# The aggregation pass of a graph-network layer: squares kept in PSUM and scanned first, stores issued in pairs, mask rows asked for at a group's head

## The reference, cut to what matters

```python
m = concat([h[dst], h[src]]) @ W_pre + b_pre
mean = segment_sum(m, dst) / deg
mean_sq = segment_sum(m * m, dst) / deg
std = sqrt(relu(mean_sq - mean * mean) + STD_EPS)
mn = segment_min(m, dst)
mx = segment_max(m, dst)
```

## Time and profile before

| | us |
|---|---|
| median of 3 runs | 4757.76 (4754.0 to 4763.07) |
| the profiled execution | 4755.44 |
| its span in the trace | 4753.5 |
| mean granted PE clock of the span | 0.706 |

### The profile page before, as it was taken

One profiled execution on the slowest core, in us unless ns is written; L12 is line 12 of the kernel. 1 busy time (PEld: TensorE's weight loads), 2 busy tenths in 40 slices (PEclk: granted clock), 3 DMA queues, 4 the chain that ended last, 5 costly groups with the idle time before them and its releaser, 6 DMA issues. The chain is left out here.

```text
span 4753.5 us, 79156 instructions
## 1 busy us (share of the span) xinstructions
PE 3229.7 (68%) x19497; PEld 2761.8 (58%) x19497; DVE 3212.5 (68%) x7496; ACT 2330.0 (49%) x4887; POOL 3360.5 (71%) x3428
## 2 busy tenths in 40 slices
PE   4888888887433334436566656665597888888886
PEld 3666666666433333335455555555465777777776
DVE  5888888887533333345677778777656676667677
ACT  4776666664200000003566666666535566666665
POOL 4777777774777777776777777777523777777774
PEclk7555555556766656667777777777798788888887
DMA  7333333331222222222677777777732333333333
GB/s 141 87 88 88 87 87 88 88 88 36 64 55 55 55 56 55 55 56 66 200 250 254 252 247 256 250 260 250 257 111 65 79 83 81 81 80 82 82 82 75
DMA packets 368299, 567.20 MB, mean 119 GB/s; under 512 B 107028, under 2 KB 171191, under 8 KB 367860
## 3 DMA queue, kind: packets, MB, share of 16 engines
q1 hardware_dynamic: 254190, 332.06, 21.5%
q0 software_dynamic: 106720, 227.64, 20.0%
q10 hardware_dynamic: 6950, 2.44, 0.2%
HBM read 328.98 MB, written 230.89 MB: 118 GB/s over the span
## 5 line engine op out<-in xcount | busy, mean ns | idle before, releaser
L2121 POOL DMA_INDIRECT m_G<-dr_tab,chunk_src x782 | 878.9, 1124 | 247.1 <-issue 238.0
L896 POOL DMA_INDIRECT e_G<-dr_tab,src_idx x830 | 792.6, 955 | 272.4 <-issue 233.5
L896 POOL DMA_INDIRECT v_G<-dr_tab,src_idx x830 | 789.4, 951 | 253.4 <-issue 245.6
L1899 POOL DMA_INDIRECT s_G<-dr_tab,chunk_src x760 | 717.3, 944 | 235.5 <-issue 226.7
L2007 PE MATMUL s_OUT<-s_G,s_S 128*128 x1664 | 378.0, 419 | 557.9 <-POOLq L1892 511.3
L2007 PEld LDWEIGHTS s_OUT<-s_G,s_S 128*128 128x128 f32 x1664 | 353.0, 323 | 582.6 <-issue 582.6
L2263 PE MATMUL m_BK<-eye,m_XT 128*128 128x128 f32 x3136 | 544.4, 342 | 170.2 <-ACT m_XB L2179 160.7
L1953 DVE TENSOR_TENSOR ACC<-ACC,s_OUT 128x129 f32 x832 | 241.4, 290 | 591.5 <-PE s_OUT L2007 474.1
L2263 PEld LDWEIGHTS m_BK<-eye,m_XT 128*128 128x128 f32 x3136 | 487.8, 181 | 217.1 <-ACT m_XB L2179 187.7
L1329 PE MATMUL e_OUT<-e_RH,e_S 128*128 128x144 f32 x1664 | 512.6, 477 | 1.9 <-DVE e_RH L1215 1.9
L2456 ACT COPY f_AT<-r_TP 128x512 f32<-128x512 f32 (+1 forms) x13 | 7.2, 554 | 943.9 <-PE r_TP L2478 943.9
(11 more groups left out here) (377 smaller groups left out, 7226.4 us busy)
## 6 DMA issues: line engine op xcount, KB each, us to landing
dr_ends<-m_XB SPq DMA_DIRECT2D x392, 512.0 KB, 4.4
e_LR<-dr_row_loc SPq DMA_DIRECT2D x104, 256.0 KB
v_LR<-dr_row_loc SPq DMA_DIRECT2D x104, 256.0 KB
m_SAME<-dr_row_same SPq DMA_DIRECT2D x98, 256.0 KB, 5.7
s_G<-dr_tab SPq DMA_DIRECT2D x1408, 0.5 KB
s_G<-dr_tab ACTq DMA_DIRECT2D x1408, 0.5 KB
e_G<-dr_tab,src_idx POOLq DMA_INDIRECT x830
v_G<-dr_tab,src_idx POOLq DMA_INDIRECT x830
```

Of the source, the lines that this page charges most:

```text
L896: pool.indirect_dma_start(out=out, out_offset=None, in_=table, in_offset=bass.IndirectOffsetOnAxis(ap=g["src_idx"][:, step:step + 1], axis ...
L1899: pool.indirect_dma_start(out=G[:, c % (RING * GROUP), 0:D], out_offset=None, in_=table[:, :], in_offset=bass.IndirectOffsetOnAxis(ap=g["c ...
L2121: pool.indirect_dma_start(out=G[:, k % Q, c % GROUP, :], out_offset=None, in_=table[:, :], in_offset=bass.IndirectOffsetOnAxis(ap=g["chunk ...
```

## The change

SQT moves from SBUF into PSUM, two banks, as one buffer where there were two. Room is made by two copy banks in place of three (`BANKS`), and by laying `UPTO` into the first of them. The squares are scanned first: the order of the parts becomes squares, sum, minimum, maximum (`TURNS`), and the semaphore counts are by place in that order (`i`) instead of by part (`m`). ACT makes `squares(k + 1)` between the copies of group `k`'s first and second part, where it made `squares(k + 2)` behind group `k`'s fourth. PE's order stays but that the `UPTO` products stand ahead of `turn(1)`. The four stores of a group go in two pairs: the first pair when the first half of the last part is copied, the second when the second half is. The mask row is asked for three groups ahead, at the group's head, once all scans of the group before are done, instead of four ahead after the group's own scans.

```diff
-    BANKS = 3
+    SUM, LEAST, MOST, SQUARES = range(PARTS)
+    TURNS = (SQUARES, SUM, LEAST, MOST)
+    BANKS = 2
...
-        SQT = fin.spare[:, 0:2 * SLOTS].rearrange("p (b c) -> p b c", b=2)
-        zero = fin.spare[:, 2 * SLOTS:2 * SLOTS + PARTS * D]
+        zero = fin.spare[:, 0:PARTS * D]
...
-        UPTO = ctx.enter_context(nc.psum_tensor(name + "UPTO", [P, 2, 3, TILES], F32))
+        SQT = ctx.enter_context(nc.psum_tensor(name + "SQT", [P, SLOTS], F32))
+        UPTO = BK[:, 0, 0:2 * 3 * TILES].rearrange("p (m c t) -> p m c t", m=2, c=3)
...
-                    if k + 4 < PICKS:
-                        sp.wait_ge(scanned, PARTS * (k + 1))
-                        same(k + 4)
+                    if 1 <= k and k + 3 < PICKS:
+                        sp.wait_ge(scanned, PARTS * k)
+                        same(k + 3)
                     for q in range(PAIRS):
-                        sp.wait_ge(xb_done, halves(k, PARTS - 1) + 2 * q + 2 if k + 1 < PICKS else halves(PICKS, 0))
+                        sp.wait_ge(xb_done, halves(k, PARTS - 1) + q // 2 + 1)
...
                 def resets(k):
                     act.wait_ge(same_in[k % 4], 16 * (k // 4 + 1))
-                    wait(act, scanned, PARTS * (k - 2) + 3)
+                    wait(act, scanned, PARTS * (k - 1))
...
                 def squares(k):
                     act.wait_ge(gt_done, k + 1)
-                    wait(act, scanned, PARTS * (k - 1))
-                    nc.scalar.activation(SQT[:, k % 2], GT[:, k % 2], ACT.Square).then_inc(sq_done, 1)
+                    wait(act, scanned, PARTS * (k - 1) + 1)
+                    nc.scalar.activation(SQT[:], GT[:, k % 2], ACT.Square).then_inc(sq_done, 1)
...
                 for k in range(PICKS):
-                    for m in range(PARTS):
-                        back(k, m)
+                    back(k, 0)
+                    if k + 1 < PICKS:
+                        squares(k + 1)
+                    for i in range(1, PARTS):
+                        back(k, i)
                     if k + 2 < PICKS:
-                        squares(k + 2)
                         resets(k + 2)
...
-                    for m, (keep, rows, joined, op) in enumerate((
-                            (same, GT[:, c], ALU.mult, ALU.add), (UP[:, c], GT[:, c], ALU.add, ALU.min),
-                            (DOWN[:, c], GT[:, c], ALU.add, ALU.max), (same, SQT[:, c], ALU.mult, ALU.add))):
-                        if m == 1:
+                    scans = {SUM: (same, GT[:, c], ALU.mult, ALU.add), LEAST: (UP[:, c], GT[:, c], ALU.add, ALU.min),
+                             MOST: (DOWN[:, c], GT[:, c], ALU.add, ALU.max), SQUARES: (same, SQT[:], ALU.mult, ALU.add)}
+                    for i, m in enumerate(TURNS):
+                        keep, rows, joined, op = scans[m]
+                        if m == LEAST:
...
                 def turn(k):
-                    wait(pe, scanned, PARTS * (k - 2) + 3)
+                    wait(pe, scanned, PARTS * (k - 1))
...
                 turn(0)
-                turn(1)
...
                 for k in range(PICKS):
-                    for m in range(PARTS):
-                        turn_back(k, m)
-                    if k + 2 < PICKS:
-                        turn(k + 2)
+                    if k + 1 < PICKS:
+                        turn(k + 1)
+                    for i in range(PARTS):
+                        turn_back(k, i)
```

More of the change, by code:

```diff
@@ L2110, in landings, with halves @@
             return 16 * (min((k + 1) * GROUP, CHUNKS) - k * GROUP + k // Q * GROUP)
-        def halves(k, m):
-            return (PARTS * k + m) * 2
+        def halves(k, i):
+            return (PARTS * k + i) * 2
         with nc.Block() as block:
@@ L2168, in squares, with back @@
                     act.wait_ge(gt_done, k + 1)
-                    wait(act, scanned, PARTS * (k - 1))
-                    nc.scalar.activation(SQT[:, k % 2], GT[:, k % 2], ACT.Square).then_inc(sq_done, 1)
-                def back(k, m):
+                    wait(act, scanned, PARTS * (k - 1) + 1)
+                    nc.scalar.activation(SQT[:], GT[:, k % 2], ACT.Square).then_inc(sq_done, 1)
+                def back(k, i):
+                    m = TURNS[i]
                     for h in range(2):
-                        n = halves(k, m) + h
+                        n = halves(k, i) + h
                         act.wait_ge(bk_done, n + 1)
-                        if m == 0 and k >= 2:
+                        if i == 0 and k >= 2:
                             for q in (2 * h, 2 * h + 1):
@@ L2184, in _ @@
                 squares(0)
-                squares(1)
                 act.wait_ge(chain, 1)
@@ L2235, in _ @@
                     dve.wait_ge(sq_done, k + 1)
-                    for m, (keep, rows, joined, op) in enumerate((
-                            (same, GT[:, c], ALU.mult, ALU.add), (UP[:, c], GT[:, c], ALU.add, ALU.min),
-                            (DOWN[:, c], GT[:, c], ALU.add, ALU.max), (same, SQT[:, c], ALU.mult, ALU.add))):
-                        if m == 1:
+                    scans = {SUM: (same, GT[:, c], ALU.mult, ALU.add), LEAST: (UP[:, c], GT[:, c], ALU.add, ALU.min),
[3 more added lines that the diff above has]
+                        if m == LEAST:
                             dve.wait_ge(reset_done, k + 1)
-                        wait(dve, scanned, PARTS * (k - 1) + m + 1)
-                        wait(dve, bk_done, halves(k - 2, m) + 2)
+                        wait(dve, scanned, PARTS * (k - 1) + i + 1)
+                        wait(dve, bk_done, halves(k - 2, i) + 2)
                         V.tensor_tensor_scan(out=XT[:, c, m, :], data0=keep, data1=rows,
@@ L2254, in turn, with turn_back @@
                     ins.then_inc(gt_done, 1)
-                def turn_back(k, m):
-                    pe.wait_ge(scanned, PARTS * k + m + 1)
+                def turn_back(k, i):
+                    m = TURNS[i]
+                    pe.wait_ge(scanned, PARTS * k + i + 1)
                     for h in range(2):
-                        n = halves(k, m) + h
+                        n = halves(k, i) + h
                         wait(pe, xb_done, n - BANKS + 1)
```

## The result

| kernel | median us | ratio to the kernel before, 95% interval |
|---|---|---|
| before | 4755.9 (4 runs) | 1 |
| after | 4618.9 (4617.0 to 4620.0, 4 runs) | 0.9709 [0.9692, 0.9726] |

The kernel is 137 us faster; 4617 was forecast. In the profiled execution the span fell from 4753.5 to 4615.9 us.

A forecast was written before the change was run, and what follows sets the result against it. POOL's gather issue was taken as the bound, 11.43 us a group falling to 9.98. From 4755.4 us, 140.7 came off and 2.3 was added: 4617 us, own range 4609 to 4626, overall range 4605 to 4650.

The forecast's parts named there:

- What bounds: POOL's issue of the PNA gathers never waits for anybody and is the bound, 11.43 us a group of 8 chunks.
- The stall: POOL's gather issues held by the scan with two SBUF inputs; squares in PSUM remove 140.7 us.
- The rival drawn from that inference: Something other than the second SBUF input holds POOL, so long issues stay: 11.43 us a group, 4758 us; chance 0.05.
- The scan of squares: On DVE, reading squares from PSUM takes this scan from 2326 ns to 2342, as the scan of sums.
- The square behind two copies: ACT copies both halves before squaring: 2.3 us more, 5.5 from gather to first scan, paid once at the end.
- its item on the end: Last gather to first ENDS gather, 27.4 us before: longer way adds 2.3, earlier stores leave less; -3 to +3, taken 0.
- its sum: Whole kernel: 4755.4 less 140.7 is 4614.7, with the 2.3 added 4617 us, 3.0% less.
- Two banks: PE and ACT with two copy banks for three: PE needs 8.8 us a group, within 9.98.
- the sum at the slowest transposes: PE's group time, 1.94 + 8 x 0.86 = 8.8 us, even with the trace's slowest transposes.
- The stores: Four stores in pairs: last lands in 10 us, ACT's buffer needed after 12.1; 2 us to spare.
- The rivals: Another bound, chance 0.10, 4637 to 4735 us; hold stays, 0.05, 4758; bunched stores slower, 0.05, 4809 at 16 us landing.
- the first rival: Two banks, square between copies or late stores make another bound: 10.2 to 11.2 us a group, 4637 to 4735; chance 0.10.

The follow-up runs named there:

- the first three experiments: Kernel after with: SQT back in SBUF, 4756.7 us; SQT in SBUF but squares' scan taking GT from PSUM, 4619.5; sums' scan reading GT's SBUF copy, 4755.8.
- first experiment: Kernel after with SQT back in SBUF, all else as changed: 4756.7 us, ratio 0.9995.

## Why the prediction was right, point by point

**What bounds.** POOL was read as the bound from its own sum of busy time and gaps, not from its 71% share of the span. The experiments bear it out from both sides: give POOL less to do, and the time falls to DVE's pace; hold it longer, and the time rises by what it is held (with both scans reading from SBUF, POOL's busy time is 978.3 us, 240 more than in the kernel after, and the time by the ratio 237 more).

**The stall.** 140.7 us were forecast and 140.9 came. The cause was read from the ends of two instructions that share no semaphore and stand 0.75 us apart every time. That was only a correlation with one scan in four; three things set that scan apart (its place in the order, its buffer, its two SBUF inputs), and the first three experiments tell them apart. Here the "Who interferes with whom" section of the Trainium skill's page "SBUF — State Buffer" agrees with the traces: by it a DVE instruction with two SBUF inputs contends with a GpSimd instruction that reads SBUF (one gather was held beside each of 96 such scans, of 98), and its inference that the writing of descriptors is left free fits the ten plain issues beside three such scans. The rival drawn from that inference failed, since the long issues went; that a gather is held because it also reads SBUF is the page's reading, and no run tests it by itself.

**The scan of squares.** 2342 ns was forecast, 2334 came, but not for the reason given. It isn't the PSUM input that goes with the longer scan but the place at a group's head, behind a wait: there a scan of squares from SBUF takes 2340 ns (first experiment), and in second place a scan of sums from PSUM takes 2321. It changed nothing in the sum.

**The square behind two copies.** Forecast as 2.3 us more from a gather to the first scan, paid once. The timeline of the kernel after shows the way: the turn, the first copy, the square and the scan.

```profile
2908.35 1.94 PE L2258 MATMUL m_GT<-eye,m_G 128*128 128x128 f32 x8 [5.21 <-DMA m_G<-dr_tab,chunk_src]
...
2911.18 0.59 ACT L2182 COPY m_XB<-m_BK 128x512 f32<-128x512 f32 x1 [5.29 <-PE m_BK L2269]
2912.03 0.59 ACT L2182 COPY m_XB<-m_BK 128x512 f32<-128x512 f32 x1 [0.27 <-PE m_BK L2269]
...
2912.51 1.02 ACT L2172 ACTIVATE m_SQT<-m_GT 128x1024 f32<-128x1024 f32 x1
...
2913.72 2.35 DVE L2248 TENSOR_TENSOR_SCAN m_XT<-m_SAME,m_XT,m_SQT 128x1024 f32<-128x1024 bf16 x1 [4.04 <-PE m_BK L2269]
```

From 2908.35 to 2913.72 are 5.4 us; 5.5 was worked out. The copies are 0.85 us apart and the square takes its 1.02 in PSUM too. The prediction isn't at one with itself here: its item on the end sets the longer way against the earlier stores and takes 0 for both together, and its sum adds the 2.3 even so. The end came out 2.0 longer. From the last gather to the end of the last copies are 21.8 us where they were 18.1, 3.7 more and not 2.3; from there to the first ENDS gather 7.7 where they were 9.4, 1.7 less, which the sum puts at nothing. That these two errors, 1.4 and 1.7, nearly cancel is luck. Why the way to the last copies grew by 3.7 was not followed up.

**Two banks.** They fit, as worked out: no row of the kernel after has POOL waiting for PE, and at DVE's 8.96 us a group they still do. PE's mean granted clock was higher in the changed pass (0.84 and 0.86 in 2600 to 2800 and 2800 to 3000 us, where before had 0.79 and 0.75), so the sum at the slowest transposes was on the safe side.

**The stores.** I put 10 us from the first request of a group to the last landing, and 2 us of cover behind it. The timeline of SP in the kernel after has the four issues of a group in about 3.2 us:

```profile
2903.35 3.19 SPq L2152 DMA_DIRECT2D dr_ends<-m_XB  x4
2906.58 1.26 SPq L2140 DMA_DIRECT2D m_SAME<-dr_row_same  x1
```

On the page of the kernel after a store lands in 3.9 us at the median, but that counts 147 of the 392 stores, each the first or second of its group; the others are matched to no landing there. By the semaphore updates in the trace, the four land 3.3, 4.5, 5.5 and 6.4 us after their own issues at the median. From a group's first request to its last landing are 8.3 us at the median, and 6.9 to 10.0 over the 98 groups. So the estimate fits the slowest group and is 1.7 us too large for an ordinary one. ACT's first copy into the same buffer began at least 2.5 us after the last landing, 5.7 at the median, so at its thinnest the cover was about what was said, and it held: ACT waits for no store in the kernel after. It held at DVE's pace too, with at least 2.2 us in the kernel with half the gathers and 0.9 in the one with plain DMAs.

**The rivals.** None of the three came. The order of the scans is the one part that, undone, gives the first rival: 10.35 us a group and 36 us.

## What to carry to other kernels

When an engine that never waits has a few instructions that are longer than the rest, look for what ends a fixed time before each of them on other engines. One engine holding up another shows so, and no list of waits named it here. A POOL gather by row number beside a DVE scan with two inputs in SBUF is such a case, and taking either input from PSUM freed it here. Before a gain on the bound is booked in full, sum each other engine for the same stretch: here the next was only 10% below, and a buffer made single would have taken a quarter of the gain had the order of the scans not been changed with it.

## What the runs showed of the hardware that was not expected

A plain DMA issue on POOL for 128 rows takes 0.545 us, one by row number 0.944 with a gap of 0.30 behind it, so that a gather by row number costs 1.25 us of POOL where plain rows cost 0.55. And POOL is not held from one two-input scan on through the next, although DVE starts the second before the first has ended by the trace (2.24 us from start to start, 2.33 long): POOL gets in between, and pays the second scan less than the first, 1.0 us and not 1.44.
